# Private PSUM banks for the last shared down product, and gated values ahead of the additions, in the last stage of a two-layer decoder

## What is computed

```python
shared = jax.nn.silu(xt @ sg_w.T) * (xt @ su_w.T) @ sd_w.T
probs = jax.nn.sigmoid(xt @ router_w.T + routing_bias)
topk_p, topk_idx = jax.lax.top_k(probs, TOP_K)          # TOP_K = 2 of E = 8
topk_p = topk_p / jnp.sum(topk_p, axis=-1, keepdims=True)
...
h = jax.nn.silu(g) * u                                   # g, u: gate and up of each expert
y = jnp.einsum('tei,ehi->teh', h, wd)
routed = jnp.einsum('te,teh->th', w, y)
return (shared + routed).reshape(orig_shape)
```

## Time and profile before

| | us |
|---|---|
| median of 3 runs | 2149.59 (2147.8 to 2155.12) |
| the profiled execution, its own time | 2145.0 |
| its span, first to last instruction | 2142.9 |

### The profile page before, as it was taken

One profiled execution on the slowest core, in us unless ns is written; L12 is line 12 of the kernel. 1 busy time (PEld: TensorE's weight loads), 2 busy tenths in 40 slices (PEclk: granted clock), 3 DMA queues, 4 the chain that ended last, 5 costly groups with the idle time before them and its releaser, 6 DMA issues. The chain is left out here.

```text
span 2142.9 us, 36053 instructions
## 1 busy us (share of the span) xinstructions
PE 1689.5 (79%) x12334; PEld 861.9 (40%) x12350; DVE 1323.9 (62%) x3599; ACT 1119.2 (52%) x1534; POOL 982.8 (46%) x987
## 2 busy tenths in 40 slices
PE   4888888888687896567777777577748779999996
PEld 2222222222254564233333333344324446666663
DVE  2767777776177996256666664454358855555545
ACT  2367776666355895245555554255445634444441
POOL 3145555431458532356777766355427741222122
PEclk9899999999798998668999977799968889999998
DMA  5332233330120000333333320322234332222216
GB/s 102 65 66 54 51 57 63 57 49 2 62 65 1 1 1 4 57 53 51 51 58 54 57 35 11 85 54 61 43 99 131 133 121 57 63 59 60 62 36 240
DMA packets 114435, 130.26 MB, mean 61 GB/s; under 512 B 22108, under 2 KB 98908, under 8 KB 114108
## 3 DMA queue, kind: packets, MB, share of 16 engines
q1 hardware_dynamic: 107780, 109.74, 25.1%
q0 software_dynamic: 6480, 18.23, 2.2%
HBM read 79.25 MB, written 47.55 MB: 59 GB/s over the span
## 5 line engine op out<-in xcount | busy, mean ns | idle before, releaser
L653 ACT ACTIVATE at_pexp<-ps 128x1024 f32<-128x1024 f32 (+3 forms) x480 | 386.3, 827 | 178.6 <-PE ps L890 177.3
L714 DVE TENSOR_REDUCE at_mx<-ps 128x1 f32<-128x512 f32 x512 | 323.9, 685 | 137.1 <-PE ps L897 135.3
L897 PE MATMUL ps<-at_ks,at_qs 48*128 48x512 f16 (+3 forms) x1024 | 284.7, 353 | 99.6 <-DVE at_mx L714 41.9
L161 PE MATMUL ps<-mo_wall,mo_xt 128*128 x1704 | 301.3, 327 | 1.1 <-issue 0.5
L890 PE MATMUL ps<-at_qs,at_ks 50*128 50x512 f16 (+4 forms) x1024 | 251.0, 343 | 20.8 <-DMA at_qs<-at_mhl 15.9
L950 PE MATMUL ps<-at_pexp,at_vaug 128*32 128x512 f32 (+4 forms) x2048 | 219.9, 522 | 11.2 <-issue 11.1
L161 PEld LDWEIGHTS ps<-mo_wall,mo_xt 128*128 128x128 f16 x1704 | 161.1, 98 | 94.5 <-issue 3.3
L2300 POOL DMA_INDIRECT mo_yd<-mo_xn,mo_idu x71 | 68.3, 962 | 275.6 <-DVE mo_xn L2557 266.8
L716 DVE CUSTOM_DVE_ANT_0 at_junk<-ps,at_lmask 128x192 bf16<-128x192 f32 x384 | 115.5, 353 | 83.3 <-PE ps L897 82.5
L897 PEld LDWEIGHTS ps<-at_ks,at_qs 48*128 48x128 f16 x1024 | 76.0, 97 | 210.6 <-DVE at_mx L714 121.8
L2360 ACT ACTIVATE mo_sg<-ps 128x512 f32<-128x512 f32 x71 | 42.5, 598 | 186.8 <-PE ps L161 186.8
(11 more groups left out here) (396 smaller groups left out, 3869.4 us busy)
## 6 DMA issues: line engine op xcount, KB each, us to landing
at_qs<-at_scratch SPq DMA_DIRECT2D x96, 128.0 KB, 7.2
at_ks<-at_scratch SPq DMA_DIRECT2D x96, 128.0 KB, 7.9
mo_xw<-mo_xs SPq DMA_DIRECT2D x71, 136.0 KB, 2.3
at_scratch<-at_qkh SPq DMA_DIRECT2D x64, 128.0 KB, 1.8
at_scratch<-at_qkl SPq DMA_DIRECT2D x64, 128.0 KB, 1.8
mo_wall<-mo_yd SPq DMA_DIRECT2D x16, 512.0 KB, 9.6
x_qs<-x_queries SPq DMA_DIRECT2D x48, 128.0 KB
mo_stage<-in_m_gate SPq DMA_DIRECT2D x9, 512.0 KB
```

The source lines that it names most:

```text
L161: last = nc.tensor.matmul(out, lhs, rhs, start=(n == 0), stop=(n == len(terms) - 1))
L653: last = act.activation(columns(pexp[:, U % 2, hh], at, n, stride, width), columns(banks(r, ST[S % 2], 2), at, n, stride, width), ACT.Exp, ...
L714: last = ve.reduce_max(out, score, AX.X)
L897: return nc.tensor.matmul(banks(r, MX[i % 2])[:, piece.at:piece.at + piece.n], qs[rows, (n // 2) % 2, h // 2, piece.idx * P:(piece.idx + 1 ...
```

## The change

Two things are changed.

1. The down product of the last batch (7) goes to banks 0 and 1 instead of 6 and 7. Its wait for `sum_ready` of batch 6 goes. In its place stand waits for `xb_ready` and `ht_ready` of the last block, the last readers of banks 0 and 1.
2. DVE's list is reordered: hidden(6, 0 to 3), add(0), hidden(7,0), add(1), hidden(7,1), add(2), hidden(7,2), hidden(7,3), add(3), add(4), add(5), add(6), finish(6), add(7), finish(7).

No instruction of an engine's work is added or taken away, and the order of the lists of TensorE, ACT, POOL and SP stays.

```diff
+        def down_bank(b):
+
+            return 0 if b == nb - 1 else DN
...
             def update(b, half):
                 ve.wait_ge(dn_done, 2 * b + half + 1)
-                return ve.scalar_tensor_tensor(out=half_x(b, half), in0=banks(r, DN + half), scalar=1.0 / WS, in1=half_x(b, half), op0=ALU.mult, op1=ALU.add)
+                return ve.scalar_tensor_tensor(out=half_x(b, half), in0=banks(r, down_bank(b) + half), scalar=1.0 / WS, in1=half_x(b, half), op0=ALU.mult, op1=ALU.add)
...
             early, late = HELD
-            hidden(early, 0)
-            hidden(early, 1)
+            for i in range(NI):
+                hidden(early, i)
             add(0)
-            hidden(early, 2)
+            hidden(late, 0)
             add(1)
-            hidden(early, 3)
+            hidden(late, 1)
             add(2)
-            hidden(late, 0)
+            hidden(late, 2)
+            hidden(late, 3)
             add(3)
-            hidden(late, 1)
             add(4)
-            hidden(late, 2)
             add(5)
             add(early)
             finish(early)
-            hidden(late, 3)
             add(late)
             finish(late)
...
                 if b == 0:
                     pe.wait_ge(w_lo, 3)
+                elif b == nb - 1:
+                    pe.wait_ge(xb_ready, NK)
+                    pe.wait_ge(ht_ready, NK)
                 elif b == FIRST:
                     pe.wait_ge(y_ready, NK)
                 else:
-                    pe.wait_ge(x_done if b < FIRST else sum_ready, 2 * (b - 1) + half + 1)
+                    pe.wait_ge(x_done, 2 * (b - 1) + half + 1)
                 for j in (2 * half, 2 * half + 1):
                     t = slice(j * P, (j + 1) * P)
-                    last = product(nc, banks(r, DN + half)[:, (j % 2) * D:(j % 2 + 1) * D],
+                    last = product(nc, banks(r, down_bank(b) + half)[:, (j % 2) * D:(j % 2 + 1) * D],
```

## The result

| | before | after |
|---|---|---|
| median of 7 runs each, us | 2149.59 | 2138.55 |
| profiled execution, its own time / span, us | 2145.0 / 2142.9 | 2145.49 / 2143.4 |

The account below looks back on a forecast made before the run. Bound: a small DVE instruction late in its list plus a half-clock down product. Last update's end 2140.34 to 2133.05 gives -7.3, stores +0.2: -7.1 us, from the median 2149.59 to 2142.5 us; range 2138.0 to 2148.0.

Parts of the forecast that it names:

- What bounds it: End of the kernel before: hidden(7,3) late in DVE's list, then a 7.99 us down product at half clock; banks alone give nothing.
- Opening: DVE, batch 6: hidden(6,2) starts at 2096.60 instead of 2101.93, hidden(6,3) at 2099.18 instead of 2105.76.
- First down product: TensorE, batch 6: starts at 2102.07 after 1.13 us idle, ends at 2107.32 instead of 2113.89, 6.6 us earlier.
- Hidden(7,1) and the rest: DVE: hidden(7,1) at 2110.74 after some 4.5 us stall, hidden(7,3) at 2116.44, finish(7) ends at 2133.05.
- Second down product: TensorE, batch 7: starts about 2119.27, ends between 2127.3 and 2129.5, off the path with 2.2 to 4.4 us of cover.
- Transfers: Loads and stores: no addition waits for its load; final stores closer together cost 0.2 us (bounds 0 and 2.1).
- A: Batch 6's down product pays 1.9 us for the gap ahead of it: gain 5.2, 2144.4 us; chance 0.12.
- C: TensorE at 1.2 GHz from 2102.07 on, DVE's stall grows: 4.7 us later than before, 2154.5 us; chance 0.04.
- B: Batch 7's down product start still tied to finish(6), at 2128.7: gain 2.9, 2146.7 us; chance 0.06.
- Its other form: DVE and POOL block each other more than the 3.83 us step contains, 4 times 1 us; same time, 2146.7 us.
- The rule of the Trainium skill: TensorE falls to half rate after idleness until busy for a while, so a gap may drop the clock; no size given.

Follow-up runs that it names:

- banks_only: Kernel before with only the private banks for the last down product, DVE's order unchanged: 50.46 us from batch 6's first gated value to the end, ratio 0.9989.
- short7_before: Kernel before, batch 7's down product without the 16 of 48 matmuls of h's low part: 48.83 us from batch 6's first gated value to the end.
- order_only: Kernel before with only DVE's new order, last down product still in banks 6 and 7: 47.41 us from batch 6's first gated value to the end, ratio 0.9990.
- again: The changed kernel measured once more without an edit: 43.19 us from batch 6's first gated value to the end, ratio to the kernel before 0.9964.
- fill: Changed kernel with add(2) ahead of hidden(7,1) and add(3) ahead of hidden(7,2): 40.72 us from batch 6's first gated value, ratio to the kernel before 0.9955.
- fill2: As fill, with add(4) whole between hidden(7,2) and hidden(7,3): 40.20 us from batch 6's first gated value to the end, one run.
- split: As fill, with additions of batches 3 and 4 taken apart into two instructions: 39.35 us from batch 6's first gated value, ratio to the kernel before 0.9942.

## Why the prediction was right, step by step

*What bounds it.* Right. The chain of waits named the last down product and behind it a gated value that stood late in DVE's list; banks_only and short7_before bear out both halves, the idle bank wait (nothing gained) and the product at the end of the path (1.6 us from its 16 matmuls).

*Opening.* hidden(6,2) was forecast at 2096.60, T + 4.17, and stands at T + 4.17; hidden(6,3) at T + 6.75, and stands at T + 6.76, released by its silu as forecast.

*First down product.* Forecast from T + 9.64 to T + 14.89, measured T + 9.65 to T + 14.90. The step taken from the pattern hidden, addition, low part (2.83 us) held. TensorE's gap ahead of it was 0.97 us and not 1.13, since the gate and up product before it ended 0.2 us later than worked out.

*Hidden(7,1) and the rest.* Forecast T + 18.31 with a stall of 4.5 us, measured T + 18.32 with 4.55. hidden(7,3): T + 24.01 forecast, T + 24.02 measured. Last update's end: T + 40.62 forecast, T + 40.49 measured; two of the additions came at 2.48 to 2.50 us and not 2.57, since 2.57 was read from add(6) before an update.

*Second down product.* Forecast start T + 26.8 (2119.27), measured T + 26.9; it ended at T + 34.0, after 7.1 us and not the 8.0 to 10.2 allowed for. The 5.2 us of cover are more than the 2.2 to 4.4 that the prediction named (its own times give 2.3 to 4.5).

*Transfers.* From the last update's end to the span's end it is 2.76 us after and 2.56 before: the 0.2 us taken. No addition waits for its load.

*The rivals.* A and C needed a lower clock at the first down product; the granted clock is 1.00 there and through batch 7's gate and up products. B is the kernel order_only: had the last product stayed tied to finish(6), the gain would have been 3.1 us, and it was forecast as 2.9. Its other form, that DVE and POOL block each other more, didn't come either: the three steps of a hidden and an addition with POOL beside them took 3.84 us each, forecast 3.83.

*The rule of the Trainium skill* ("TensorE: Matmul & The Clock Gate", the section on the HAM clock gate), by which the array falls to half rate after idleness: the trace agrees where the idleness was 4.07 us (clock 0.50 for 3.4 us of the last product) and shows no fall after 0.97 us.

*What was off.* The size in the run times: median 2138.55 against 2142.5, inside the range of 2138.0 to 2148.0, but by 0.6 us only, and 2137.83 would have been outside. That it fell inside is partly luck: the prediction took 2149.59 as its base, and in three sets of runs the kernel before had medians of 2149.59, 2151.42 and 2148.21. The tail's gain was right to 0.1 us; the rest of the 11.4 us is not seen in the tail, and its size is within what the stretch ahead of T does by itself. In the eleven traces T lies between 2088.17 and 2100.15, 12 us apart, while the tail of one program (after, again) agrees to 0.1 us, and its last update ends at T + 40.49 in both. The first layer-norm statistics of the expert stage start at 1591.8 in the trace of after; this is the row of them, then that of order_only:

```profile
L123 DVE BATCH_NORM_STATS2 mo_stats<-X x32: 402/409/422, 1591.8 to 1703.1; 128x6 f32<-128x256 f32 x32
```

```profile
L123 DVE BATCH_NORM_STATS2 mo_stats<-X x32: 401/410/425, 1580.3 to 1691.6; 128x6 f32<-128x256 f32 x32
```

From there to T it is 508.35 us in the one and 508.3 in the other, so the 11.5 us between these two arose in the stages ahead of the experts. (In fill that stretch took 2 us more.) What makes it there was not tried and stays open. The prediction took the runs' scatter into its range and chances, but a gain of 0.33% in the presence of it can't be placed on either side of 0.3% with much confidence; 0.56 for "faster" says that.

## What to carry to other kernels

When the chain ends in an engine that waited for a small step of another engine, look at that engine's own list: a long "issue" gap may be a short instruction queued behind work that nobody waits for. Two waits of one instruction have to go together: taking away the earlier of them gave nothing here, and taking away the later only about as much as lies between them (3.4 us before, from the end of the update at 2127.55 to the product at 2131.64; 3.1 were gained). After such a move the wait turns up at the next product in the chain; a piece of movable work that fit in it was free (fill), and one that didn't returned only part of what it filled (fill2).

## What the runs showed of the hardware

The granted clock can fall in the middle of a product: after 4.07 us of idleness the last product ran its first 7 matmuls at 1.00 (2127.10 to 2127.80) and the next 18 at 0.50. In fill, after 4.08 us of idleness, its first 17 were at 0.50 at once:

```profile
2124.90:2128.30 3.40, 3.40 (x17) 0.50 1.08 383
```

The whole product took 8.0 us in fill and 7.1 in the kernel after. So the start of such a product is no sign of the clock that it will get.

A half addition with two SBUF inputs that was issued while POOL subtracted took 1.96 to 2.18 us instead of 1.21, and POOL's subtraction took 1.40 instead of 1.15 where the addition was first. That the addition waits for POOL to finish is read from the ends: the one issued at 2108.86 in the kernel after (POOL: 1.40 us from 2108.34) and those at 2110.03 and 2119.09 in split each ended 1.08 us after POOL, nearly the length of a half alone. The same wait cost nothing where DVE would have idled anyway (the one at 2110.03).
